# Four graph phases joined into one program on one Trainium2 core, and one phase's scores computed in strips of columns

## The reference

```python
# block 0, two layers l: undirected graph attention
u = where(j >= i, (h @ (h @ W_left[l].T).T), (h @ (h @ W_right[l].T).T)) / sqrt(384)   # by adjacency
attention = exp(u) * adj / (sum(exp(u) * adj) + 1e-10)
h = relu(layer_norm(attention @ (h @ W_lin[l].T + b_lin[l])))
# blocks 1 and 2: attention with 12 heads, bias 2*adj or adj
p = softmax(q @ k.T * 384**-0.5 + bias);  out = (p @ v) @ Wo.T + bo
# block 3, two layers: directed, scores from h alone
u = h @ h.T / sqrt(384);  attn = normalised softmax(u) * adj
ctx = (attn above diagonal) @ (h Wl) + diag * (h Ws) + (attn below diagonal) @ (h Wr)
h = relu(layer_norm(ctx))
```

## Time and profile before

| | |
|---|---|
| median of 3 runs | 3056.74 us |
| profiled execution | 3056.15 us |
| its span, first to last instruction | 3054.4 us |
| TensorE busy | 2807.4 us (92%) |
| VectorE, GpSimd, ScalarE busy | 2043.4, 1311.5, 1214.8 us |
| mean granted TensorE clock | 0.983 |

### The profile page before, as it was taken

How to read it: one execution, slowest core, us unless ns; L and a number is a source line. 1 busy time by engine, 2 the same in 40 slices (tenths; PEclk the granted TensorE clock), 3 DMA queues, 4 the chain that set the end, 5 groups by cost and what they waited for, 6 DMA issues and landing times. The chain is left out here.

```text
span 3054.4 us, 82121 instructions
## 1 busy us (share of the span) xinstructions
PE 2807.4 (92%) x32768; PEld 2576.5 (84%) x32768; DVE 2043.4 (67%) x3932; ACT 1214.8 (40%) x1941; POOL 1311.5 (43%) x2315
## 2 busy tenths in 40 slices
PE   6999999999968999999879999999699999999997
PEld 6888888888868888888768888888588888888886
DVE  4666666666656777777657777777567777777776
ACT  3333333333333333333333333333345454545443
POOL 1212222221213333333323333333267878878787
PEclk9999999999989999999989999999799999999999
DMA  4111111111121111111121111111211111112120
GB/s 137 39 63 50 57 57 57 57 38 61 52 84 37 45 45 45 45 45 45 45 66 46 44 45 44 45 44 47 77 32 46 52 52 52 52 35 68 34 69 31
DMA packets 116482, 158.81 MB, mean 52 GB/s; under 512 B 8000, under 2 KB 112320, under 8 KB 116416
## 3 DMA queue, kind: packets, MB, share of 16 engines
q1 hardware_dynamic: 116416, 157.88, 16.0%
HBM read 107.52 MB, written 50.33 MB: 52 GB/s over the span
## 5 line engine op out<-in xcount | busy, mean ns | idle before, releaser
L162 PE MATMUL ps<-t_hi,w_hi 128*128 128x256 f32 x2304 | 662.7, 288 | 51.7 <-DVE t_lo L900 49.1
L164 PE MATMUL ps<-t_hi,w_lo 128*128 128x256 f32 x2304 | 647.8, 281 | 0.0
L163 PE MATMUL ps<-t_lo,w_hi 128*128 128x256 f32 x2304 | 647.1, 281 | 0.0
L162 PE MATMUL ps<-w_hi,t_hi 128*128 128x384 f32 x1536 | 534.9, 348 | 3.7 <-ACT q L845 3.6
L164 PE MATMUL ps<-w_hi,t_lo 128*128 128x384 f32 x1536 | 517.7, 337 | 0.0
L163 PE MATMUL ps<-w_lo,t_hi 128*128 128x384 f32 x1536 | 517.6, 337 | 0.0
L162 PEld LDWEIGHTS ps<-t_hi,w_hi 128*128 128x128 f32 x2304 | 436.7, 190 | 83.2 <-DVE t_lo L900 58.2
L163 PEld LDWEIGHTS ps<-t_lo,w_hi 128*128 128x128 f32 x2304 | 437.0, 190 | 0.0
L164 PEld LDWEIGHTS ps<-t_hi,w_lo 128*128 128x128 f32 x2304 | 436.7, 190 | 0.0
L814 POOL TENSOR_TENSOR e<-e,factor 128x512 f32<-128x512 f32 x192 | 195.1, 1043 | 448.6 <-DVE factor L938 448.6
L1196 POOL TENSOR_TENSOR hw<-hw,w_row 128x192 f32<-128x192 f32 x512 | 348.1, 711 | 53.8 <-ACT hw L1277 52.3
(11 more groups left out here) (150 smaller groups left out, 6272.9 us busy)
## 6 DMA issues: line engine op xcount, KB each, us to landing
x_after<-xout SPq DMA_DIRECT2D x96, 384.0 KB, 2.5
xin<-x_after SPq DMA_DIRECT2D x96, 384.0 KB, 3.4
xin<-in_x SPq DMA_DIRECT2D x32, 384.0 KB, 4.2
x<-in_x SPq DMA_DIRECT2D x32, 384.0 KB, 3.6
x<-x_after SPq DMA_DIRECT2D x32, 384.0 KB, 3.6
out<-xout SPq DMA_DIRECT2D x32, 384.0 KB, 2.8
w_raw<-in_w SPq DMA_DIRECT2D x4, 2304.0 KB, 8.8
adjin<-in_adj SPq DMA_DIRECT2D x32, 256.0 KB, 3.7
```

Source lines behind the costliest of these rows:

```text
L162: nc.tensor.matmul(out, lhs_hi, rhs_hi, start=(k == 0), stop=False)
L163: nc.tensor.matmul(out, lhs_hi, rhs_lo, start=False, stop=False)
L164: last = nc.tensor.matmul(out, lhs_lo, rhs_hi, start=False, stop=(k == len(terms) - 1))
```

## The change

The four phases become one program without a wait of all engines between them. Their buffers are cut from one shared memory per stream (class `Memory`), and `started(i, before)` marks waits that a phase's first iteration now needs for the phase before. `run_stages` is taken apart: round 0 of phase 0 (`run_first`), rounds 1 to 15 of each phase (`run_middle`), a round between two phases (`run_between`) whose lists `BETWEEN` mix the late stages of one with the first stages of the next, and the last late stages (`run_last`). In these lists w0 to w5 are the splits of a weight matrix of the new phase, on ScalarE and VectorE. `SLOTS` says in which of six places a matrix stands, `weights_free` waits for the last use of the place, and `PRESPLIT` lists matrices that are split after round 1 of the phase before. The raw weights have four places instead of six, so matrices 4 and 5 are fetched after the first two are split. In SyncE's program the parameters and weights of the next phase are fetched after the loads of round 1, and those loads wait for the last store of the phase before. In phase 3 the last norm is written into the output buffer. The scores of phase 0 are made in strips: each matmul has 32 stationary columns and only the 96 moving ones that the strip needs, so a stage has 24 matmuls in place of 12, on four strips of 32 output partitions in place of two of 64; for this the left and right products of a graph lie side by side (`mlr`).

```diff
+SLOTS = ((0, 1, 2, 3, 4, 5), (0, 1, 2, 3), (4, 5, 0, 1), (2, 3, 4, 5, 0, 1))
+PRESPLIT = {1: (), 2: (0, 1), 3: (0, 1)}
...
+BETWEEN = [
+    [
+        "mr_1.1' aT_1.0' agg_1.0' u_1.1' lin_1.1' hT.0 aT_1.1' agg_1.1' q.0 hT.1 v.0 k.0 scores.0 q.1 v.1",
+        "w0 w1 aT_0.1' z_0.1' w2 ml_1.0' mr_1.0' hT_1.1' soft_1.0' ml_1.1' aT_1.0' mr_1.1' z_1.0' w3 "
+        "soft_1.1' norm.0 norm.1 hT.0 aT_1.1' z_1.1' q.0 hT.1 k.0 q.1",
+        "w0 w1 lin_1.0' stat.1 att_1.0' stat.0 sum_1.0' w2 soft_1.1' agg_1.0' w3 att_1.1' lin_1.1' sum_1.1' "
+        "hT.0 ln_1.0' gain.0' beta.0' out.0' agg_1.1' hT.1 ln_1.1' gain.1' beta.1' out.1' v.0 soft.0 fac.0 "
+        "v.1",
+        "stat.1 stat.0 agg_1.0' agg_1.1' xb.0 bias.0 p.0",
+    ],
+    [
+        "k.1' pt0.0' pt2.0' pt1.0' pv0.0' pv1.0' pv2.0' hT.0 scores.1' q.0 out.0' v.0 k.0 pt0.1' pt1.1' "
+        "pt2.1' pv0.1' pv1.1' pv2.1' hT.1 scores.0 q.1 out.1' v.1",
+        "exp.0' k.1' pt0.0' pt2.0' w2 pt1.0' norm.0 pv.0' hT.0 w3 q.0 exp.1' k.0 pt0.1' pt1.1' pt2.1' norm.1 "
+        "pv.1' hT.1 q.1",
+        "stat.0 w2 pv.0' hT.0 soft.1' fac.1' out.0' stat.1 w3 v.0 pv.1' hT.1 soft.0 out.1' fac.0 v.1",
+        "stat.0 xb.1' bias.1' p.1' stat.1 xb.0 bias.0 p.0",
+    ],
+    [
+        "k.1' pt0.0' pt2.0' pt1.0' pv0.0' scores.1' pv1.0' pv2.0' out.0' hT_0.0 pt0.1' pt1.1' u_0.0 pt2.1' "
+        "pv0.1' pv1.1' pv2.1' w0_0.0 out.1' hT_0.1 w1_0.0 aT_0.0 w2_0.0 u_0.1 agg_0.0 w0_0.1 w1_0.1 hT_1.0 "
+        "aT_0.1 w2_0.1 u_1.0 agg_0.1 w0_1.0 w1_1.0",
+        "exp.0' pt0.0' k.1' pt2.0' w2 w3 w4 norm.0 pt1.0' pv.0' exp.1' hT_0.0 pt0.1' pt1.1' pt2.1' pv.1' "
+        "swap_0.0 soft_0.0 tiny_0.0 w0_0.0 norm.1 w5 hT_0.1 w1_0.0 swap_0.1 on_0.0 soft_0.1 tiny_0.1 w0_0.1 "
+        "w1_0.1 hT_1.0",
+        "stat.0 soft.1' pv.0' fac.1' stat.1 out.0' split_0.0 pv.1' soft_0.0 w2 att_0.0 diag_0.0 split_0.1 "
+        "sum_0.0 w3 out.1' aT_0.0 w2_0.0 soft_0.1 w4 att_0.1 diag_0.1 agg_0.0 ln_0.0 sum_0.1 aT_0.1 w2_0.1 "
+        "split_1.0 soft_1.0 agg_0.1 ln_0.1 att_1.0 w5",
+        "xb.1' bias.1' adj_1.0 stat.0 adj_0.1 p.1' stat.1 adj_0.0 on_0.0 w0_0.0 diag_0.0 w1_0.0 on_0.1 "
+        "agg_0.0 w0_0.1 diag_0.1 w1_0.1 agg_0.1",
+    ],
+]
...
+def run_first(order, todo):
+
+    for stage, s, late in order:
+        if not late:
+            todo[stage](s, 0)
+
+
+def run_middle(eng, order, todo, meanwhile=None):
+
+    order = [(todo[stage], s, late) for stage, s, late in order]
 
     def round_of(r):
         for stage, s, late in order:
-            if not isinstance(r, int) or 0 <= r - late < ITER:
-                stage(s, r - late)
-    round_of(0)
+            stage(s, r - late)
     round_of(1)
+    if meanwhile is not None:
+        meanwhile()
     with eng.Fori(2, ITER) as r:
         round_of(r)
-    round_of(ITER)
+
+
+def run_between(line, ended, begun):
+
+
+    for word in line.split():
+        if word[0] == "w" and word[1:].isdigit():
+            begun["weights"](int(word[1:]))
+            continue
+        stage, s = word.rstrip("'").rsplit(".", 1)
+        if word.endswith("'"):
+            ended[stage](int(s), ITER - 1)
+        else:
+            begun[stage](int(s), 0)
+
+
+def run_last(order, todo):
+
+    for stage, s, late in order:
+        if late:
+            todo[stage](s, ITER - 1)
...
+def started(i, before):
+
+
+    return before is not None and isinstance(i, int) and i == 0
+
+
+def weights_free(eng, phases, phase, m):
+
+
+    for past in (phase - 1, phase - 2):
+        if past >= 0 and SLOTS[phase][m] in SLOTS[past]:
+            user = phases[past].weight_users[SLOTS[past].index(SLOTS[phase][m])]
+            for s in range(STREAMS):
+                eng.wait_ge(phases[past].pe_done[s], phases[past].PE[s](user, ITER - 1))
+            return
+
+
+def split_hi(act, g, phases, phase, m):
+
+    if m == 0:
+        act.wait_ge(g.weights_in[phase], 16)
+    if m == STAGED:
+        act.wait_ge(g.more_weights_in[phase], 16)
+    weights_free(act, phases, phase, m)
+    nc = g.nc
+    nc.scalar.activation(g.w_hi[:, SLOTS[phase][m]], g.w_raw[:, m % STAGED], ACT.Copy).then_inc(g.hi_split[phase], 1)
+
+
+def split_lo(dve, g, phases, phase, m):
+
+    dve.wait_ge(g.hi_split[phase], m + 1)
+    nc = g.nc
+    at = SLOTS[phase][m]
+    nc.vector.tensor_tensor(g.w_lo[:, at], g.w_raw[:, m % STAGED], g.w_hi[:, at].bitcast(F32),
+                            ALU.subtract).then_inc(g.lo_split[phase], 1)
...
+def raw_weights(sp, g, phase):
+
+    sp.wait_ge(g.hi_split[phase - 1], len(SLOTS[phase - 1]))
+    sp.wait_ge(g.lo_split[phase - 1], len(SLOTS[phase - 1]))
+    sp.dma_start(g.w_raw[:], g.weights[phase][:, :STAGED]).then_inc(g.weights_in[phase], 16)
+
+
+def more_raw_weights(sp, g, phase):
+
+    if len(SLOTS[phase]) > STAGED:
+        n = len(SLOTS[phase]) - STAGED
+        sp.wait_ge(g.hi_split[phase], n)
+        sp.wait_ge(g.lo_split[phase], n)
+        sp.dma_start(g.w_raw[:, 0:n], g.weights[phase][:, STAGED:]).then_inc(g.more_weights_in[phase], 16)
...
     if phase == 0:
         for s in range(STREAMS):
             load(s, 0)
-    if x_again:
+        for dst, src in ph.params:
+            sp.dma_start(dst, src).then_inc(sems.params_in, 16)
+    if ph.reload:
         for s in range(STREAMS):
+            ph.x_space(sp, s)
             x_again(s, 0)
-    for dst, src in rows:
-        sp.dma_start(dst, src.partition_broadcast(P)).then_inc(sems.params_in, 16)
-    if n_mats > STAGED:
-        sp.dma_start(g.w_raw[:, STAGED:], g.weights[phase][:, STAGED:]).then_inc(g.more_weights_in[phase], 16)
-
-    if phase + 1 < len(g.weights):
-        sp.wait_ge(g.hi_split[phase], n_mats)
-        sp.wait_ge(g.lo_split[phase], n_mats)
-        nxt = g.weights[phase + 1]
-        sp.dma_start(g.w_raw[:, :STAGED], nxt[:, :STAGED]).then_inc(g.weights_in[phase + 1], 16)
-
-    def store_and_reload(s, i):
-        store(s, i)
-        if x_again and (not isinstance(i, int) or i + 1 < ITER):
-            x_again(s, i + 1)
+    if phase == 0:
+        more_raw_weights(sp, g, 0)
     for s in range(STREAMS):
-        load(s, 1, 0)
+        if before is not None:
+            sp.wait_ge(before.sems.stored[s], 16 * ITER + 1)
+        load(s, 1)
+    if nxt < len(SLOTS):
+        for dst, src in phases[nxt].params:
+            sp.dma_start(dst, src).then_inc(phases[nxt].sems.params_in, 16)
+        raw_weights(sp, g, nxt)
     with sp.Fori(2, ITER) as i:
         for s in range(STREAMS):
             store_and_reload(s, i - 2)
-            load(s, i, i - 1)
+            load(s, i)
+    if phase and nxt < len(SLOTS):
+        more_raw_weights(sp, g, nxt)
     for s in range(STREAMS):
         store_and_reload(s, ITER - 2)
-        if phase + 1 < len(g.sources):
+        if nxt < len(SLOTS):
             sp.wait_ge(sems.stored[s], 16 * (ITER - 2) + 1)
-            load(s, 0, ITER - 1, of=phase + 1)
+            load(s, 0, of=nxt)
     for s in range(STREAMS):
         store_and_reload(s, ITER - 1)
...
+        b.mlr = m.wide[:, 4 * T * FEAT:6 * T * FEAT].rearrange("p (g k j) -> p g k j", k=2, j=NODES)
...
+                b = bufs[s]
+                pe.wait_ge(act_done[s], AC[s].all(i, (f"ml_{l}", 0), (f"mr_{l}", 0)))
+                for half in range(2):
+                    for c in range(C):
+                        for t in range(T):
+                            for blk in range(2):
+                                first_token = t * P + half * NODES + blk * HD
+                                to = t * NODES + blk * HD
+                                wanted = slice(blk * HD, blk * HD + 3 * HD)
+                                mm = nc.tensor.matmul(
+                                    b.ps[to:to + HD, 2 - 2 * l, half * P:(half + 1) * P][:, wanted],
+                                    b.hT[:, c, first_token:first_token + HD],
+                                    b.mlr[:, c * T * 2 + t * 2 + half].rearrange("p k j -> p (k j)")[:, wanted],
+                                    start=(c == 0), stop=(c == C - 1), tile_position=(0, to))
+                mm.then_inc(pe_done[s], 1)
...
+            if started(i, before):
+                act.wait_ge(before.pe_done[s], before.PE[s](before.h_read, ITER - 1))
...
+            elif started(i, before):
+                pe.wait_ge(before.act_done[s], before.AC[s]("z_1", ITER - 1))
...
+                if l == 1:
+                    dve.wait_ge(sems.stored[s], 16 * i + 1)
+                    if started(i, before):
+                        dve.wait_ge(before.sems.stored[s], 16 * ITER + 1)
...
+        def run(eng, k, weights=None):
+
+            todo = [dict(ph.stages[k](eng), weights=weights and (lambda m, n=n: weights(n, m)))
+                    for n, ph in enumerate(phases)]
+            run_first(phases[0].orders[k], todo[0])
+            for n, ph in enumerate(phases):
+                def meanwhile(to=n + 1):
+                    if weights:
+                        for m in PRESPLIT[to]:
+                            weights(to, m)
```

(54 more changed lines are left out.)

1994 lines of the change are left out of this document (968 added, 1026 removed).

## The result

The changed kernel takes 2966.31 us (median of 4 runs, 2966.07 to 2966.42) against 3057.03 us for the kernel before in the same comparison: a ratio of 0.9703, 95% interval 0.9687 to 0.9718. It is faster by 90.7 us; the prediction said 2960 (2940 to 3000), the forecast case.

The account below looks back on a forecast made before the run. The prediction took TensorE's own work to bound the rounds, with idle time at the three seams. Its terms, 20 + 29 + 22 + 30 - 4.7 = 96 us off 3054.4, plus 1.8 around it, gave 2960 us, range 2940 to 3000.

Parts of the forecast that it names:

- the forecast case: Whole kernel: the summed savings hold and the time falls within 2942 to 2980 us; chance 70%.
- Part 1: Phase 0's scores in four strips: stage u from 1.53 to 1.23 us, 64 stages, about 20 us saved.
- all in TensorE's path: Phase 0's scores: all 64 stages count in full on TensorE, 64 x 0.30 = 19 us, called 20.
- The first rival: Phase 0's scores: four strips run one after another, 3.9 us a stage, +152 us, total about 3133; chance 4%.
- Part 2: Seam between phases 1 and 2: 41.8 us against 70.7, 29 us saved, bounds 24 to 32.
- Part 3: Seam between phases 0 and 1: 37.9 us against 60.0, 22 us saved, bounds 14 to 26.
- Part 4: Seam between phases 2 and 3: 61.3 us against 91.1, 30 us saved, bounds 22 to 35.
- 4.6 + 2.0 + 0.6 + 2: Seam 2 to 3, TensorE idle: ScalarE's splits and h 4.6 us, o_hi/o_lo chain 2.0, stream 1's p 0.6, fill 2.
- the clock row near 1.00 throughout: Sign expected in the profile after: granted clock near 1.00 across the whole span, seams included.
- Part 5: Weight splits ahead, after round 1 of phases 1 and 2: some 2.3 us each paid, 4.7 lost, bounds 0 and 7.
- At nothing: Shared buffers, earlier parameter loads, SyncE's new waits, the start and the end: all priced at zero.

Follow-up runs that it names:

- unmixed kernel: Changed kernel, still one program, but each seam ends all late stages of the old phase before splits and new stages: 3033.67 us, ratio 0.9918.
- strips alone: Kernel before with only the four-strip scores of phase 0 and their mlr layout, four programs and seams kept: 3041.73 us, ratio 0.9948.
- e11_placed: Changed kernel with presplits moved: ScalarE's two behind hT.1 of round 1, VectorE's two behind stat.0 of round 2: 2961.64 us, ratio 0.9686.
- e6_scores_early: Changed kernel, seam 2 to 3 reordered: TensorE's scores.1' ahead of pt1.0' and pv, ScalarE's queue reordered too: 2962.59 us, ratio 0.9687.

## Why the prediction was right, and where not

**Bound and method.** TensorE's work set the rounds, and the walk through the in-order lists gave the seams: 38.9, 42.2 and 63.2 us against 37.9, 41.8 and 61.3. No wait of TensorE at a seam passed 5 us.

**Part 1** was right in the stage (1.20 us, forecast 1.23) and too large in the sum: 13.8 to 15.5 us against 20. The failed step is "all in TensorE's path": what stands behind u, agg and the transpose of e, is fed by VectorE on its own schedule. The ends of a stage's neighbours should have been in the sum (agg waits 20.7 us over the phase before too). The mechanism behind the stage's 1.23 us held: four strips run side by side with 128 rows, each at its own pace of 82 ns for 96 columns, 0.86 ns a column where the sum took 0.79. The first rival's price of 3.9 us a stage holds by the same pace (48 x 82 ns), and its condition was not met.

**Part 2** held: 28.5 us of 29. **Part 3** held: 21.1 of 22. **Part 4**, 27.9 of 30: the work was right, and the waits 2.16 + 4.63 + 1.62 = 8.4 us where 4.6 + 2.0 + 0.6 + 2 = 9.2 were expected, though differently shared. The term left out is the clock. The prediction took for granted that mixed seams keep it up ("the clock row near 1.00 throughout"); two of three don't (windows of after at the three seams, columns as above):

```profile
877.00:887.00 10.00, 8.02 (x152) 7.57 (x150) 8.40 (x8) 1.20 (x2) 4.25 (x4) 1.00 0.29 88
1475.00:1485.00 10.00, 9.38 (x167) 8.75 (x152) 8.39 (x7) 3.77 (x6) 1.41 (x2) 0.66 0.17 49
2095.00:2105.00 10.00, 3.67 (x72) 3.46 (x73) 9.86 (x9) 3.85 (x5) 0.42 (x2) 0.50 0.06 23
```

At 0.50 the 18 records of out.0' took 5.85 us, where a stretch at 1.00 has 3.4; at seam 1 to 2 q.0 took 5.42 instead of 3.45. The page's row of 40 slices, 74 us each, is too coarse to show it.

**Part 5**: the rounds around the splits are 3.7 and 4.2 us longer than two steady ones, 1.0 and 0.3 in the kernel before, so 6.6 us against 4.7. By its own numbers the sum should have said less: 2.7 us of w_lo with 1.0 to spare leaves 1.7 for each pair, 3.4 in all, and not 2.3 and 4.7. The step that failed is the reason: it priced a place in VectorE's queue, and what was paid is in the main GpSimd's p stretched beside w_lo (2.1 of 3.3 us in phase 1) and the clock behind it.

**At nothing:** the start gave 1.5 us and phase 3's rounds 1.3, neither in the sum; phase 3's also appear in the unmixed kernel (730.7) and not in strips alone (732.2), so they come with the shared program, by what of it wasn't tried.

Together: 5 us too much for part 1, 3.5 for the seams, 2 for part 5, less some 4 of gains not forecast (start, phase 3, steady attention rounds of 38.15 instead of 38.20): 96 becomes 89.8. That the whole came within 7 us of the forecast time is in part luck, since terms on both sides were missed.

## What to carry to other kernels

An idle stretch between two phases is filled by stages of the other phase, not by taking the barrier away: here 67 us against 8. To price a faster stage, look at what each stage behind it waits for, and take the gain only as far as that allows. A reordering that gives the forecast time is not yet explained: look whether it came from the stretch that was edited, and put two such edits together, since e11_placed and e6_scores_early each gave 4 to 5 us and together no more. Compare the edited stretch with the same stretch of every kernel that leaves it alone. Matmuls for different strips of columns are best issued in turn: strip by strip, the same 48 records took 2.05 us instead of 1.20.
